# A fused cross-attention and mixture-of-experts kernel: top two by VectorE's top-eight instructions, biases added by DMAs, a block count by a shift, a floor column in the mask, and result loads for batches 0 to 2 ahead of the rest

## What is computed

```python
q, k, v = heads(layernorm(x) @ Wq.T + bq), heads(ctx @ Wk.T + bk), heads(ctx @ Wv.T + bv)   # 16 heads of 8
attn = softmax(where(mask == 0, -inf, q @ k.T / sqrt(8)))      # mask (512, 154)
x = x + (attn @ v) @ Wo.T + bo
xf = layernorm(x)                                              # 2048 tokens
logits = xf @ Wg                                               # 16 experts
gates = softmax of the two largest logits, 0 for the others
y = sum over e of (silu(xf @ W1[e] + b1[e]) * (xf @ W11[e] + b11[e]) @ W2[e] + b2[e]) * gates[:, e]
z = silu(xf @ Ws1 + bs1) * (xf @ Ws11 + bs11) @ Ws2 + bs2      # a shared expert of width 512
out = x + y + z
```

## Time and profile before

| | us |
|---|---|
| median of 3 runs | 316.48 (315.83 to 317.02) |
| the profiled execution | 317.54 |
| its span in the trace | 315.7 |

### The profile page before, as it was taken

How to read it: one execution, slowest core, us unless ns; L and a number is a source line. 1 busy time by engine, 2 the same in 40 slices (tenths; PEclk the granted TensorE clock), 3 DMA queues, 4 the chain that set the end, 5 groups by cost and what they waited for, 6 DMA issues and landing times.

```text
span 315.7 us, 6054 instructions
## 1 busy us (share of the span) xinstructions
PE 274.9 (87%) x1836; PEld 207.8 (66%) x1836; DVE 215.1 (68%) x713; ACT 149.6 (47%) x313; POOL 139.0 (44%) x227
## 2 busy tenths in 40 slices
PE   7678899988989999998998889999699999999800
PEld 7655455745656556564564467899589999999800
DVE  2856666774786779766797458883257787787806
ACT  3323687644656456564654654422145545545300
POOL 4555433421531234845338402745016576675720
PEclk9797999997999999999999999999999999999975
DMA  6999920000000098000001100118615959685147
GB/s 216 372 369 396 406 102 4 0 0 2 0 1 2 0 354 317 27 27 17 2 0 35 37 1 2 51 34 239 215 41 159 313 163 275 225 267 189 52 139 284
DMA packets 24080, 42.12 MB, mean 133 GB/s; under 512 B 2689, under 2 KB 11777, under 8 KB 24049
## 3 DMA queue, kind: packets, MB, share of 16 engines
q1 hardware_dynamic: 21520, 36.52, 34.4%
q0 software_dynamic: 2528, 5.22, 4.8%
HBM read 27.00 MB, written 14.73 MB: 132 GB/s over the span
## 4 chain that ended last, share of the span: by engine, by line
PE 62%; DVE 20%; DMA 6%; issue 5%; POOL 4%; ACT 2%; POOLq 0%; DVEq 0%; ACTq 0%; SPq 0%
DVE mpad L572 7%; PE ps L1432 6%; PE ps L1438 6%; PE ps L1449 6%; PE ps L1208 5%; PE ps L1166 4%; PE ps L1194 4%; PE ps L1204 4%; PE ps L1167 4%; PE ps L1179 3%; POOL slot_rows L868 3%; PE ps L1192 3%; PE ps L1222 2%; PE ps L1116 2%; PE ps L1117 2%
## 5 line engine op out<-in xcount | busy, mean ns | idle before, releaser
L572 DVE TENSOR_REDUCE mpad<-ps 128x2 f32<-128x308 f32 x128 | 55.3, 472 | 34.1 <-PE ps L1167 33.7
L818 POOL TENSOR_SCALAR ks<-k_stack,cst 128x160 fp32r<-128x160 f32 x64 | 31.2, 501 | 83.0 <-DVE k_stack L557 83.0
L930 POOL DMA_INDIRECT result_rows<-yo,dest x47 | 44.9, 956 | 38.3 <-DVE yo L792 35.3
L995 ACT ACTIVATE pf<-ps 128x512 f32<-128x512 f32 x80 | 46.5, 596 | 16.9 <-PE ps L1208 10.8
L1167 PE MATMUL ps<-ks,qs 96*128 96x308 f32 x128 | 46.0, 416 | 0.0
L1166 PE MATMUL ps<-mq_b,identb 128*128 128x308 bf16 x128 | 38.8, 309 | 6.6 <-DVE mpad L572 6.0
L868 POOL DMA_INDIRECT slot_rows<-xr,slot x32 | 31.5, 985 | 14.4 <-issue 14.0
L1194 PE MATMUL ps<-qs,ks 128*128 128x512 f32 x64 | 37.6, 589 | 0.0
L1166 PEld LDWEIGHTS ps<-mq_b,identb 128*128 128x128 bf16 x128 | 12.5, 98 | 34.4 <-issue 28.9
L1103 ACT ACTIVATE e_s<-ps,wu 128x128 f32<-128x128 f32 x62 | 19.4, 363 | 22.0 <-PE ps L1432 22.0
L1449 PE MATMUL ps<-wd,e_h 128*128 (+1 forms) x188 | 28.7, 277 | 0.6 <-DVE yo L792 0.6
(11 more groups left out here) (190 smaller groups left out, 612.9 us busy)
## 6 DMA issues: line engine op xcount, KB each, us to landing
wu<-w_biased SPq DMA_DIRECT2D x31, 322.0 KB, 4.7
wr<-w_up SPq DMA_DIRECT2D x1, 5152.0 KB, 24.9
w_biased<-wr SPq DMA_DIRECT2D x1, 5152.0 KB, 16.7
slot_rows<-zero SPq DMA_DIRECT2D x1, 3120.0 KB, 27.4
xg<-slot_rows SPq DMA_DIRECT2D x12, 260.0 KB, 3.6
wd<-w_down SPq DMA_DIRECT2D x1, 2048.0 KB, 11.8
xo<-result_rows SPq DMA_DIRECT2D x4, 512.0 KB, 5.4
out<-xs SPq DMA_DIRECT2D x4, 256.0 KB, 2.3
```

Of the source, the lines that this page charges most:

```text
L572: dve.tensor_reduce(mpad[:, m % 2, q, 96 + 2 * a:98 + 2 * a], ps[:, KS_ + a, 0:2 * SK].rearrange("p (c k) -> p c k", c=2), AX.X, ALU.max, ...
L930: pool.indirect_dma_start(out=result_dram[:, :], out_offset=bass.IndirectOffsetOnAxis(ap=dest[:, n:n + 1], axis=0), in_=yo[:, n % 4, :], i ...
L995: act.activation(pf[:, n % RP, :], ps[:, ST_ + n % 2, :], ACT.Exp, scale=DK ** -0.5).then_inc(exp_done, 1)
```

## The change

- `pick`: instead of two rounds of largest value, comparison and first index, four `max` (one a tile; the eight largest of 16 logits), four `max_index` (their places), one copy of the first two places to float, and two comparisons with the expert numbers. `sel` and the difference of the two logits are step 3. Only the ends of the steps are linked.
- `add_bias`, `empty_rows` and `add_biases` leave VectorE. GpSimd issues two adding DMAs: `bo` on all of `xs` at the head of (0,3), after a wait for the last `norm_rows`; and `bs2` on all sixteen `b2` rows at the head of (1,1). The first `add_attention` waits for the former, SyncE's copy of `wr` for the latter.
- `slots` step 1: the count plus 127, shifted right by 7, in three operations over 16 elements.
- The mask gets two more columns of half the masking value, so that products and maxima have 2 x 156 = 312 columns; a row without a key gets its maximum from there.
- After the first 40 tiles in the run's order (`SETTLED`) have landed SyncE loads the results of batches 0 to 2; after all 47 it loads batch 3 in two halves of 256 KB. Adds and stores go by these five pieces (`PIECES`).

```diff
...
 RUN = TILES - 1
+SETTLED = NE + 2 * (TOK - S) // P
+PIECES = tuple((QT * c, QT) for c in range(B - 1)) + ((NT - QT, QT // 2), (NT - QT // 2, QT // 2))
...
                              ).then_inc(ld_u[d % RW], 16)
-            sp.wait_ge(biased, NG)
+            sp.wait_ge(biased, 16)
...
                     d += 1
+            pairs = result_dram[SLOTS:SLOTS + 2 * TOK, :].rearrange("(p t k) d -> p t k d", t=NT, k=2)
+            def load_results(i):
+                t, count = PIECES[i]
+                sp.dma_start(xo[:, t:t + count, :, :], pairs[:, t:t + count, :, :]).then_inc(ld_r[i], 16)
+            for r in range(4):
+                sp.wait_ge(returned[r], (SETTLED - r + 3) // 4 * 16)
+            for i in range(B - 1):
+                load_results(i)
...
                 sp.wait_ge(returned[r], (RUN - r + 3) // 4 * 16)
-            pairs = result_dram[SLOTS:SLOTS + 2 * TOK, :].rearrange("(p t k) d -> p t k d", t=NT, k=2)
-            for c in range(B):
-                sp.dma_start(xo[:, QT * c:QT * c + QT, :, :], pairs[:, QT * c:QT * c + QT, :, :]).then_inc(ld_r[c], 16)
-            for c in range(B):
-                sp.wait_ge(out_done, c + 1)
-                sp.dma_start(out[:, QT * c:QT * c + QT, :], xs[:, QT * c:QT * c + QT, :]).then_inc(stored, 16)
+            for i in range(B - 1, len(PIECES)):
+                load_results(i)
+            for i, (t, count) in enumerate(PIECES):
+                sp.wait_ge(out_done, i + 1)
+                sp.dma_start(out[:, t:t + count, :], xs[:, t:t + count, :]).then_inc(stored, 16)
...
             sp.wait_ge(zeroed, 16)
-            sp.wait_ge(stored, 16 * B)
+            sp.wait_ge(stored, 16 * len(PIECES))
...
                 return four(v, b).unsqueeze(2).to_broadcast([P, QT, NE])
-            desc = cst[:, C_DESC:C_DESC + NE].unsqueeze(1).to_broadcast([P, QT, NE])
-            def largest(b, of, m, one):
-                tiles = slice(QT * b, QT * b + QT)
-                link(dve.tensor_reduce(four(m, b), of[:, tiles, :], AX.X, ALU.max))
-                link(dve.tensor_tensor(one[:, tiles, :], of[:, tiles, :], four_rows(m, b), ALU.is_equal))
-            def first_of_largest(b, one):
-                tiles = slice(QT * b, QT * b + QT)
-                link(dve.tensor_tensor(one[:, tiles, :], one[:, tiles, :], desc, ALU.mult))
-                link(dve.tensor_reduce(four(mi, b), one[:, tiles, :], AX.X, ALU.max))
-                link(dve.tensor_tensor(one[:, tiles, :], four_rows(mi, b), desc, ALU.is_equal))
...
             def pick(b, step):
-                tiles = slice(QT * b, QT * b + QT)
+                tiles = range(QT * b, QT * b + QT)
+                cols = slice(QT * b, QT * b + QT)
...
                     dve.wait_ge(lg_done, b + 1)
-                    largest(b, lg, m1, one1)
+                    for i, t in enumerate(tiles):
+                        last = dve.max(top[:, i, :], lg[:, t, :])
+                    link(last)
...
                 elif step == 1:
-                    first_of_largest(b, one1)
+                    for i, t in enumerate(tiles):
+                        last = dve.max_index(place[:, i, :], top[:, i, :], lg[:, t, :])
+                    link(last)
+                    link(dve.tensor_copy(choice[:, :, :], place[:, :, 0:2]))
...
                 elif step == 2:
-                    link(dve.scalar_tensor_tensor(out=top[:, tiles, :], in0=one1[:, tiles, :], scalar=-BIG,
-                                                  in1=lg[:, tiles, :], op0=ALU.mult, op1=ALU.add))
-                    largest(b, top, m2, one2)
-                elif step == 3:
-                    first_of_largest(b, one2)
+                    ids = cst[:, C_TILE:C_TILE + NE].unsqueeze(1).to_broadcast([P, QT, NE])
+                    for k, one in enumerate((one1, one2)):
+                        last = dve.tensor_tensor(one[:, cols, :], choice[:, :, k:k + 1].to_broadcast([P, QT, NE]), ids,
+                                                 ALU.is_equal)
+                    link(last)
...
                 else:
-                    dve.tensor_tensor(sel[:, tiles, :], one1[:, tiles, :], one2[:, tiles, :], ALU.add).then_inc(sel_done, 1)
-                    dve.tensor_tensor(four(m2, b), four(m2, b), four(m1, b), ALU.subtract).then_inc(ex_in, 1)
+                    dve.tensor_tensor(sel[:, cols, :], one1[:, cols, :], one2[:, cols, :], ALU.add).then_inc(sel_done, 1)
+                    dve.tensor_tensor(m2[:, cols].unsqueeze(2), top[:, :, 1:2], top[:, :, 0:1], ALU.subtract).then_inc(ex_in, 1)
...
                 tiles = slice(QT * b, QT * b + QT)
-                full = [P, NE, NE]
...
                 elif step == 1:
-                    link(dve.tensor_tensor(scr[:, :, :], cum[:, b + 1, :].unsqueeze(2).to_broadcast(full),
-                                           cst[:, C_T128:C_T128 + NE].unsqueeze(1).to_broadcast(full), ALU.is_gt))
-                    link(dve.tensor_reduce(nb[:, b + 1, :], scr[:, :, :], AX.X, ALU.add))
+                    link(dve.tensor_scalar(full_up[:, :], cum[:, b + 1, :], 1.0, float(P - 1), ALU.max, ALU.add))
+                    link(dve.tensor_scalar(full_up[:, :], full_up[:, :], 7, None, ALU.logical_shift_right))
+                    link(dve.tensor_copy(nb[:, b + 1, :], full_up[:, :]))
...
                 dve.wait_ge(ld_m, 32)
-                for dst, src in ((mq_b[:, :, :], mq_raw[:, :, :]), (mk_b[:, :], mk_raw[:, :])):
+                dve.memset(mq_b[:, :, SK:SKM], MASKED / 2)
+                for dst, src in ((mq_b[:, :, 0:SK], mq_raw[:, :, :]), (mk_b[:, :], mk_raw[:, :])):
...
                 last.then_inc(wlo_done, 1)
-            def empty_rows():
-                link(dve.tensor_reduce(row_nan[:, :], mq_b[:, :, :], AX.X, ALU.max))
-                link(dve.tensor_scalar(row_any[:, :], row_nan[:, :], 0.0, None, ALU.is_equal))
-                link(dve.reciprocal(row_inv[:, :], row_any[:, :]))
-                link(dve.tensor_tensor(row_nan[:, :], row_any[:, :], row_inv[:, :], ALU.mult))
-                link(dve.tensor_scalar(row_nan[:, :], row_nan[:, :], -1.0, None, ALU.add))
-            def add_bias(q):
-                rows = xs[:, :, :].rearrange("p (b q) d -> p b q d", q=QT)[:, :, q, :]
-                return dve.scalar_tensor_tensor(out=rows, in0=rows, scalar=row_nan[:, q:q + 1],
-                                                in1=bor[:, :].unsqueeze(1).to_broadcast([P, B, D]),
-                                                op0=ALU.add, op1=ALU.add)
...
                     dve.tensor_reduce(mpad[:, m % 2, q, 96 + 2 * a:98 + 2 * a],
-                                      ps[:, KS_ + a, 0:2 * SK].rearrange("p (c k) -> p c k", c=2),
+                                      ps[:, KS_ + a, 0:2 * SKM].rearrange("p (c k) -> p c k", c=2),
...
                 reach(dve, x1_mm, b, 1, nb + 1)
+                if b + nb == 0:
+                    dve.wait_ge(bo_added, 16)
...
                                   ALU.add).then_inc(x1_done, 1)
-            def add_biases(i):
-                rows = wr[:, 4 * i:4 * i + 4, WB:WB + D]
-                dve.tensor_tensor(rows, rows, bsr[:, :].unsqueeze(1).to_broadcast([P, 4, D]), ALU.add).then_inc(biased, 1)
...
                         block_statistics(1)
-                    if b == 1 and g == 0:
-                        dve.wait_ge(ld_wr, 32)
-                        add_bias(0)
-                        add_bias(1)
...
                         block_statistics(2)
-                    if b == 0 and g == 1:
-                        empty_rows()
-                    if b == 1 and g == 0:
-                        add_bias(2)
-                        add_bias(3)
...
                         pick(b - 1, 3)
-                        pick(b - 1, 4)
...
                         batch_norm(b, -1)
-                    if b == 1:
-                        if g == 0:
-                            dve.wait_ge(ld_b, 16)
-                            dve.wait_ge(ld_d, 32)
-                        add_biases(g)
...
             read_logits(last)
-            for step in range(5):
+            for step in range(4):
...
                     meta(n // 4 + 1)
-            for c in range(B):
-                dve.wait_ge(ld_r[c], 16)
-                rows = xs[:, QT * c:QT * c + QT, :]
-                link(dve.tensor_tensor(rows, rows, xo[:, QT * c:QT * c + QT, 0, :], ALU.add))
-                dve.tensor_tensor(rows, rows, xo[:, QT * c:QT * c + QT, 1, :], ALU.add).then_inc(out_done, 1)
+            for i, (t, count) in enumerate(PIECES):
+                dve.wait_ge(ld_r[i], 16)
+                rows = xs[:, t:t + count, :]
+                link(dve.tensor_tensor(rows, rows, xo[:, t:t + count, 0, :], ALU.add))
+                dve.tensor_tensor(rows, rows, xo[:, t:t + count, 1, :], ALU.add).then_inc(out_done, 1)
...
                 for g in range(NG):
+                    if b == 0 and g == 3:
+                        pool.wait_ge(ld_wr, 32)
```

(24 more changed lines are left out.)

9 lines of the change are left out of this document (4 added, 5 removed).

## The result

| kernel | median us | lowest to highest | executions |
|---|---|---|---|
| before | 316.74 | 315.83 to 317.02 | 4 |
| changed | 307.77 | 306.81 to 309.81 | 4 |

The ratio is 0.9734, with a 95% interval of 0.968 to 0.9789. The profiled execution of the changed kernel took 307.24 us (span 305.4), 10.3 less than that of before. The same two kernels ran again in three sets beside the experiments: all 18 executions of the changed kernel have the median 308.0 (305.55 to 310.23), and the medians of before are 314.64, 315.34 and 317.15. Set by set the medians differ by 9.0, 5.4, 6.8 and 10.3 us; the profiled pair, with 10.3, stands at the upper end.

What follows compares the result with a forecast made beforehand. It took TensorE, with 62% of the chain, as the main bound, beside VectorE's 20%. Terms -4.4 - 0.8 - 0.55 + 0.5 - 4.4 = -9.65 took 317.5 to 307.9 us, median 306.9; range 304 to 315.

Steps and rivals of the forecast that it cites:

- Biases on VectorE: Attention groups of batch 1: removing the bias operations saves 2.9 and 0.7 us, the vanished clock dip 0.85; -4.4 in all.
- Biases on GpSimd: Two adding DMAs in (0,3) and (1,1) fit into GpSimd's slack of about 7.5 and 9.6 us: cost 0.
- G: Unknown time one adding DMA holds GpSimd: bounds 0.96 and 15.3 us, taken as 6 to 8.
- Rivals 1 and 2: Adding DMAs hold GpSimd 15.3 us or more (median 320.4, chance 0.14), or 8 to 13 (311 us, chance 0.15).
- Pick: Expert choice: -1.0 us where TensorE waited for `sel` in (3,3), +0.1 each in (1,3) and (2,3); -0.8 in all.
- Rival 3: Expert choice: `max_index` runs at the pace of linked operations, +5.1 us, so 312.0; chance 0.13.
- Shift: Block count in `slots`: 0.62 us instead of 0.90, twice on the path behind attention; -0.55 us.
- Floor column: Mask, maxima and matmuls at 312 instead of 308 columns: 4 ns a maximum, partly on the chain; +0.5 us.
- Tail: Kernel's end: early result loads and halved last loads bring the end from 315.7 to 311.2 us; -4.4 taken.
- Rival 4: Kernel's end: early loads slow the last sends' landings and stores stand before the last ones; half of 4.4, 309.1; chance 0.08.

Runs made afterwards that it cites:

- the sixteen DMAs: Changed kernel with the DMA that adds `bo` cut into sixteen of one tile each, 128 runs of 512 bytes a DMA: 318.73 us, ratio 1.0109.
- biases back: Changed kernel with the biases added by VectorE as before and without the two adding DMAs: 312.04 us, ratio 0.9905.

## Why the prediction was right, point by point

The forecast was 307.9 for the profiled execution and 306.9 for the median; measured were 307.24 and 307.77, and 308.0 over all executions. The mechanism held and most of the terms came out, but some of the agreement is luck: a tail term 1.0 too large in the profiled pair is offset by 1.2 us at the start that aren't the change's, and inside the bias term two errors cancel.

- **Biases on VectorE: -4.4, measured -4.37 in the profiled pair.** (1,0) came to 8.68, 0.04 from (2,0). The split was wrong, though. The operations are worth 2.9 to 3.05 in all (2.4 in (1,0), 0.6 from `add_biases`), where 2.9 and 0.7 were taken, and the clock 1.5, not 0.85: the prediction counted the one pair at half speed that the chain showed, while by the windows the clock was low from about 72 to 75 us, partly in (1,0) and mostly in (1,1). And this part is won only against executions of before in which the clock dips. The medians of before differ by 2.5 us between the sets, and this may be a part of the reason; that stays open.
- **Biases on GpSimd: cost 0, right; G = 6 to 8, measured 2.37 and 2.12.** The term was mis-sized. It lies near the lower bound, not near the middle: most of the 0.96 us for 128 rows is start-up. The reading of the slack, which made the cost 0 for any G up to 7.5, was borne out by the sixteen DMAs, which overran it and paid. The Trainium skill, "DMA: Bandwidth & Descriptors", section "Anatomy of one DMA", has many descriptors go out before their cost shows. The trace agrees in part: 16 times the runs took 2.6 times as long, but by that rule the prediction had G at about 1, and it is 2.37. Rivals 1 and 2, at G of 8 to 15.3, are excluded.
- **Pick: -0.8, measured -1.4.** In (3,3) -1.06 against -1.0. In (1,3) and (2,3) the prediction had +0.1 each, and it is -0.16 each by undoing it (-0.1 in the profiled pair). The four `max` come to 0.32 us on the chain of (1,3) instead of 0.5 and `max_index` to 0.60 instead of 0.85. Rival 3, `max_index` at the linked pace, is excluded by starts 0.06 to 0.09 apart. Two of the figures around it don't come out: eleven linked steps in 2.89 us are 0.263 each, not 0.257, and the rival's loss of 0.8 in (3,3) has `max` at that pace as well; by `max_index` alone it is 0.3.
- **Shift: -0.55, measured -0.24 to -0.34.** The shift is 0.07 us longer than taken, so that each count saves 0.21 and not 0.28; that both counts lie on the path isn't borne out.
- **Floor column: +0.5, measured +0.25.** The 4 ns a maximum were right (472 to 476); less of the maxima and matmuls lies on the chain than taken, and which of the two isn't shown.
- **Tail: -4.4, measured -3.42 in the profiled pair, -2.5 in the mean of the four profiles from the first expert on and -2.7 from the last pair of `e_h` on.** The failing step is the time of the last send. The prediction left it where it was; behind the last pair of `e_h` it starts 4.7, 7.0, 6.2 and 5.5 us in the four profiles, where it starts 3.9 to 4.0 before and in the kernels in which no tile waits for a `yo` buffer. The terms behind it held: the load of 256 KB took 3.18 us for 3.3, four adds 1.7, then 2.3 to the end. Rival 4 named this mechanism, early loads slowing the sends' landings, with half of 4.4 lost; lost were 1.0 in the profiled pair and 1.7 to 1.9 in the mean. So the forecast's tail held only in part, and rival 4 in part as well. The trace of before already had the sign of it, sends that land in up to 6.1 us beside the loads of weights. Its other half, early stores standing before the last loads' adds, didn't come up on the chain.
- **The start, -1.23, was not foreseen** and isn't the change's.

Summed anew from the runs: -3.0 for the bias operations, -1.5 for the clock where it dips, -1.4 for the pick, -0.3 for the shift, +0.25 for the column, -2.7 for the tail: -7.2 to -8.7. The medians of the sets differ by 5.4 to 10.3.

No kernel beat the changed one beyond its interval; the one with eight buffers has the lowest ratio of its set, 0.9704 against 0.9773, and that is open.

## What to carry to other kernels

When work moves to an engine with idle time, compare its unknown price with the slack ahead of the next thing somebody waits for, not with zero: here the slack was 7.5 us; a price of 2.4 was free, one of 14.5 was not. A transfer moved ahead of the last writes wasn't free here either, though no wait named it: it lengthened their landings, and with four buffers that came back as a wait on the computing engine. Before, sends beside the loads of weights were already late; a landing time read where nothing else runs, like the 2.4 us taken here, isn't the one to sum with. And where a stretch of before ran at a lower granted clock, say how often it does, since only those executions can win it back.

## What the runs showed of the hardware

- A GpSimd DMA that adds 1 MB to SBUF in 2048 runs of 512 bytes holds the engine 2.37 us (2.12 the other one) and lands in 11.3 us (9.8); of sixteen with 128 runs each, one behind the other, each holds it 0.90 us.
- `max` over 16 elements shows as 0.16 us; `max_index` as two instructions, 0.07 to 0.09 and 0.17 us, issued so close that a pair costs about 0.15. The Trainium skill, "VectorE: DVE Perf Modes", section "Two Vector instructions with no wait between them", has the value load and the index search as two instructions too; the trace agrees, with the rows at 173.42 and 173.50.
- Sends of 128 rows that land in 2.2 us alone take 3.9 to 6.5, by the chains, beside 1.5 MB of loads from the same memory, and 3.7 to 6.1 beside the last loads of expert weights (before).
- Behind nearly the same idle stretch of TensorE, the granted clock fell to 0.50, from 2.4 to 1.2 GHz, for some 3 us in one profile (before) and stayed at 1.00 in another (biases back).
- The first group of attention starts 31.3 to 32.9 us into the span in kernels that are alike up to there.
